# Moving eight of sixteen low-part subtractions from VectorE to GpSimd in a routed expert MLP

## The reference

```python
# block 1: four experts, chosen by token id; Wg = Wu = Wd = ctx_2048 (4 x 512 x 512)
for e in range(E):
    g = jax.nn.silu(jnp.einsum('bsd,fd->bsf', hidden_states, Wg[e]))
    u = jnp.einsum('bsd,fd->bsf', hidden_states, Wu[e])
    y = jnp.einsum('bsf,df->bsd', g * u, Wd[e])
    out = jnp.where((expert_ids == e)[..., None], y, out)
x = x + jnp.tanh(g_xattn[0]) * experts(_layernorm(x), ids, ctx_2048, ctx_2048, ctx_2048)
# block 2: ternary MLP of 1408 hidden channels, scaled per channel
x = x + jnp.tanh(g_ffn[0]) * ffn(_layernorm(x), gate_w, up_w, down_w, gate_s, up_s, down_s)
```

## Time and profile before

| | |
|---|---|
| median of 3 runs | 389.07 us |
| the profiled execution | 389.44 us |
| its span | 387.7 us |
| PE busy | 373.1 us, 96% of the span |
| VectorE busy | 243.5 us, 63% |
| ScalarE busy | 147.1 us, 38% |
| GpSimd busy | 81.8 us, 21% |

### The profile page before, as it was taken

One profiled execution on the slowest core, in us unless ns is written; L12 is line 12 of the kernel. 1 busy time (PEld: TensorE's weight loads), 2 busy tenths in 40 slices (PEclk: granted clock), 3 DMA queues, 4 the chain that ended last, 5 costly groups with the idle time before them and its releaser, 6 DMA issues.

```text
span 387.7 us, 5617 instructions
## 1 busy us (share of the span) xinstructions
PE 373.1 (96%) x1757; PEld 303.1 (78%) x1757; DVE 243.5 (63%) x455; ACT 147.1 (38%) x265; POOL 81.8 (21%) x108
## 2 busy tenths in 40 slices
PE   3999999999999999999999999999999999999992
PEld 2477788888888878888888888888888888888891
DVE  6888856667877678778847255747246757222253
ACT  4355556565545346422332223332222332222220
POOL 7523443434352120010002101002101001200011
PEclk9999999999999999999999999999999999999997
DMA  6775666663221126333201322200232300100011
GB/s 221 258 253 191 248 216 253 210 216 102 89 68 68 56 86 216 97 119 81 83 0 54 135 80 83 71 11 31 88 124 62 101 27 27 81 0 0 0 41 73
DMA packets 21905, 40.91 MB, mean 106 GB/s; under 512 B 2672, under 2 KB 8816, under 8 KB 21888
## 3 DMA queue, kind: packets, MB, share of 16 engines
q1 hardware_dynamic: 17536, 26.50, 21.3%
q0 software_dynamic: 4352, 14.19, 9.8%
HBM read 28.36 MB, written 12.32 MB: 105 GB/s over the span
## 4 chain that ended last, share of the span: by engine, by line
PE 93%; DVE 3%; POOL 1%; issue 1%; ACT 0%; DVEq 0%; POOLq 0%
PE bank L1149 40%; PE bank L1045 26%; PE bank L1156 20%; PE bank L1031 2%; PE bank L1060 2%; PE bank L1073 1%; POOL minus_j L362 1%; PE bank L1021 0%; DVE rows L934 0%; PE bank L1012 0%; DVE tmp L927 0%; DVE xn L927 0%; DVE is_low L647 0%; PE bank L1083 0%; DVE sh L882 0%
## 5 line engine op out<-in xcount | busy, mean ns | idle before, releaser
L1149 PE MATMUL bank<-work,wgu 128*128 (+1 forms) x736 | 167.3, 380 | 0.0
L1149 PEld LDWEIGHTS bank<-work,wgu 128*128 128x128 f32 x736 | 133.9, 188 | 27.1 <-issue 0.5
L1045 PE MATMUL bank<-work,parts 128*128 (+1 forms) x432 | 110.7, 402 | 0.8 <-ACT parts L463 0.2
L1045 PEld LDWEIGHTS bank<-work,parts 128*128 128x128 f32 x432 | 78.5, 188 | 20.0 <-issue 2.9
L1156 PE MATMUL bank<-work,hp 128*128 128x512 f32 x352 | 87.2, 390 | 0.2 <-DVE hp L886 0.2
L1156 PEld LDWEIGHTS bank<-work,hp 128*128 128x128 f32 x352 | 65.7, 188 | 14.4 <-DVE hp L886 0.6
L867 DVE SCALAR_TENSOR_TENSOR sh<-bank,gs,sh 128x512 f32<-128x512 f32 x42 | 31.5, 749 | 55.6 <-PE bank L1149 55.6
L567 ACT ACTIVATE hp<-sh 128x512 fp32r<-128x512 f32 x42 | 26.6, 634 | 78.7 <-DVE sh L867 78.7
L562 ACT ACTIVATE sh<-bank,gs 128x512 f32<-128x512 f32 x42 | 28.9, 689 | 71.6 <-PE bank L1149 68.8
L391 POOL TENSOR_TENSOR rstd<-ve,half 128x1 f32<-128x1 f32 x31 | 18.1, 583 | 124.3 <-DVE ve L708 124.3
L446 POOL DMA_INDIRECT out<-rows,oidx x16 | 16.2, 1011 | 128.0 <-DVE rows L934 105.8
(11 more groups left out here) (132 smaller groups left out, 267.4 us busy)
## 6 DMA issues: line engine op xcount, KB each, us to landing
wraw<-guT SPq DMA_DIRECT2D x8, 704.0 KB
ctx_in<-ctxT SPq DMA_DIRECT2D x4, 1024.0 KB, 6.1
rows<-x_rows SPq DMA_DIRECT2D x8, 512.0 KB, 4.4
turned_rows<-xn SPq DMA_DIRECT2D x12, 256.0 KB, 2.7
rows<-turned_rows SPq DMA_DIRECT2D x12, 256.0 KB, 2.7
checked<-dwT SPq DMA_DIRECT2D x11, 256.0 KB
rows<-dwT SPq DMA_DIRECT2D x11, 256.0 KB, 2.9
rows<-x,gidx POOLq DMA_INDIRECT x19
```

Source lines behind the costliest of these rows:

```text
L1045: mm = pe.matmul(out_ps[:, :], part(s)[:, c * P:(c + 1) * P], ctx_w(e, c, w), start=n == 0, stop=n == last)
L1149: mm = pe.matmul(out_ps[:, tiles.start * P:tiles.stop * P], wgu[:, row + h, w, c * P:(c + 1) * P], moving, start=n == 0, stop=n == last)
```

## The change

Eight of the sixteen low parts are made by GpSimd: (e, c) = (0,3), (1,3), all four of expert 2, and (3,0), (3,1). VectorE keeps (0,0), (0,1), (0,2), (1,0), (1,1), (1,2), (3,2), (3,3). The instruction is the same, a `tensor_tensor` subtraction of 128 x 512. GpSimd's go into its queue after gather 3 (one), after gather 4 (one), after gather 5 and ahead of inverse_std(3) (four), and after store 0 (two). On VectorE, step 1 begins with three subtractions, step 2 has none, and step 3 has two, which moved behind h_lo(2). TensorE and SyncE wait on two semaphores in place of one.

```diff
+ON_POOL = [(0, 3), (1, 3), (2, 0), (2, 1), (2, 2), (2, 3), (3, 0), (3, 1)]
+ON_VECTOR = [(e, c) for e in range(EXPERTS) for c in range(KC) if (e, c) not in ON_POOL]
...
-            sp.wait_ge(S["ctx_lo"], EXPERTS * KC)
+            sp.wait_ge(S["ctx_lo"], len(ON_VECTOR))
+            sp.wait_ge(S["pool_ctx_lo"], len(ON_POOL))
...
+            def ctx_lo(n):
+                e, c = ON_POOL[n]
+                pool.wait_ge(S["ctx_hi"], KC * e + c + 1)
+                pool.tensor_tensor(ctx_w(e, c, 1), ctx_in[:, e, c, :], ctx_w(e, c, 0).bitcast(F32),
+                                   ALU.subtract).then_inc(S["pool_ctx_lo"], 1)
...
             gather(3)
+            ctx_lo(0)
             inverse_std(1)
             gather(4)
+            ctx_lo(1)
             inverse_std(2)
             pool.wait_ge(S["early_row"], 16)
             gather(5)
+            for n in range(2, 6):
+                ctx_lo(n)
             inverse_std(3)
             pool.wait_ge(S["tables_ready"], 2)
             pool.wait_ge(S["rows_ready"], 1)
             store(0)
+            for n in range(6, len(ON_POOL)):
+                ctx_lo(n)
...
             def step_with_ctx(k):
-                ctx_lo(KC * k, KC * (k + 1))
+                if k == 1:
+                    ctx_lo(3, 6)
                 norm(k + 1, ring_slot(k + 1))
                 h_lo(k - 1)
+                if k == 3:
+                    ctx_lo(6, 8)
                 hidden(k)
...
-            ctx_lo(2, KC)
+            ctx_lo(2, 3)
             norm(1, ring_slot(1))
...
-                    if n >= 2 * KC and ctx_ready:
-                        pe.wait_ge(S["ctx_lo"], ctx_ready - KC + c + 1)
+                    if n >= 2 * KC and ctx_of is not None:
+                        pe.wait_ge(*ctx_low_ready(ctx_of, c))
```

More of the change, by code:

```diff
@@ L246, in build @@
             z_done y_done silu_ready h_ready ht_done early_index early_row xn_out xq_in xt_ready hhi_ready hlo_ready u_done rows_ready
-            scaled gates_ready dsb_ready ctx_hi ctx_lo out_stored  held
+            scaled gates_ready dsb_ready ctx_hi ctx_lo pool_ctx_lo out_stored  held
             check_landed sums_done checks_done loose_step loose_ready loose_counted flag_ready
@@ L778, in ctx_lo @@
             def ctx_lo(n_from, n_to):
-                for n in range(n_from, n_to):
-                    e, c = n // KC, n % KC
-                    dve.wait_ge(S["ctx_hi"], n + 1)
+                for e, c in ON_VECTOR[n_from:n_to]:
+                    dve.wait_ge(S["ctx_hi"], KC * e + c + 1)
                     dve.tensor_tensor(ctx_w(e, c, 1), ctx_in[:, e, c, :], ctx_w(e, c, 0).bitcast(F32),
@@ L1032, in turn_x, with ctx_low_ready, expert_product @@
                 mm.then_inc(S["xt_done"], 1)
-            def expert_product(out_ps, part, e, hi_ready, lo_ready, ctx_ready=None):
+            def ctx_low_ready(e, c):
+                made, sem = (ON_POOL, "pool_ctx_lo") if (e, c) in ON_POOL else (ON_VECTOR, "ctx_lo")
+                return S[sem], made.index((e, c)) + 1
+            def expert_product(out_ps, part, e, hi_ready, lo_ready, ctx_of=None):
                 last = len(PASSES) * KC - 1
@@ L1050, in expert, with first_product @@
                 return pe.value_load(tiles[0:1, 0, ds(k, 1)], min_val=0, max_val=EXPERTS - 1)
-            def first_product(k, e=None, ctx_ready=None):
+            def first_product(k, e=None, ctx_of=None):
                 e = expert(k) if e is None else e
                 expert_product(z_ps, tile_x, e, (S["xhi_ready"], k + 1),
-                               (S["xlo_ready"], k + 1), ctx_ready).then_inc(S["z_done"], 1)
+                               (S["xlo_ready"], k + 1), ctx_of).then_inc(S["z_done"], 1)
             def turn_h(k):
@@ L1078, in _ @@
             keep_busy(3)
-            first_product(0, 0, ctx_ready=KC)
+            first_product(0, 0, ctx_of=0)
             pe.wait_ge(S["low_ready"], 3)
@@ L1091, in _, with expert_step @@
             turn_h(0)
-            def expert_step(k, e=None, e_before=None, ctx_ready=None, first=None):
-                first_product(k, e, ctx_ready)
+            def expert_step(k, e=None, e_before=None, ctx_of=None, first=None):
+                first_product(k, e, ctx_of)
                 turn_x(k + 1)
@@ L1106, in _ @@
             for k in range(1, EXPERTS):
-                expert_step(k, *experts_at(k), ctx_ready=KC * (k + 1))
+                expert_step(k, *experts_at(k), ctx_of=k)
             with pe.Fori(EXPERTS, 15) as k:
```

## The result

The changed kernel takes 394.75 us (median of 4 runs, 394.34 to 395.38) against 389.1 us before: ratio 1.0151, 95% interval 1.0136 to 1.0165, so 5.65 us slower. The forecast was 387.3 us.

The account below looks back on a forecast made before the run. TensorE was taken as the bound, with 3.02 us to win in first products 0 to 3. Gains of 0.19 us, then totals of 0.58, 1.28 and 1.78, gave 387.3 us from the median; range 386.6 to 389.2.

Parts of the forecast that it names:

- The price of one subtraction: Time of one 128 x 512 subtraction on GpSimd, estimated from memset and select: 1.3 us, low end 0.88, high end 2.1.
- Step 0: Product 0, with (0,3) on GpSimd and (0,2) waiting for it: last matmul at 19.34 instead of 19.53, gain 0.19 us.
- Step 1: Product 1, with (1,3) on GpSimd: ends at 25.58 us instead of 26.16, total gain 0.58.
- The first rival: GpSimd's (2,0) goes ahead of norm(2), which stands still 1.3 us: total gain only 0.62, 388.45 us; chance 0.32.
- Step 2: Product 2, with no VectorE subtraction ahead of it: its 0.70 us over go, total gain 1.28 us.
- the forecast slack: Margin for norm(3), held behind GpSimd's four until 31.7 us, with turn_x(3) due at 32.1: 0.4 us.
- Step 3: Product 3, with (3,0) and (3,1) on GpSimd: a stall of 0.1 remains of 0.61; gain 0.5 us, total 1.78.
- The carry-over: After the start, TensorE is busy 234.83 of 235.00 us, so the rest takes over any gain or loss one for one.

## Why the prediction was wrong

- **The price of one subtraction** was right: 1.28 us on GpSimd (1.255 to 1.306) for a forecast 1.3, worked out from a memset and a select.
- **Step 0** came near in its total, and partly by luck: product 0 ended at 19.94 instead of 20.03, 0.09 us early for a forecast 0.19. It was shorter than forecast (3.19 us, forecast 3.35), but began 0.26 us later than before (16.75 against 16.49); over the traces of all these kernels its start lies between 16.09 and 17.00, which the sum held fixed. (0,2) did not meet (0,3), which ended at 18.18, ahead of it. In five of the six traces in which product 0 began at 16.09 to 16.16 they met, as forecast: (0,2) took 0.77 us in one and 0.92 or 0.93 in four. (A reading was slightly off: the power instruction of the earlier trace rows ended 0.43 us after the first subtraction, 19.30 against 18.87, and not 0.5. The sum does not use it.)
- **Step 1 is where it failed.** The sum let "the three subtractions of VectorE end at 22.84 + 0.60 + 0.60 + 0.68 = 24.72", so it put the wait of (1,2) at nothing and gave no reason. The first rival had GpSimd ahead of norm(2), for one instruction of 1.3 us. I looked for a meeting only at norm(2): by the sum (1,2) began at 24.04, ahead of the end of gather 5 at 24.2 to 24.39. In fact (1,2) was the victim, took 5.86 us and ended at 29.99: being shown to begin first did not protect it, and the hold lasted for the row of four. Forecast: 0.58 us gained by the end of product 1, or by the rival 0.58 lost. Measured: turn_x(2) 5.18 us late.
- **The clock** was in no term. After the wait of 5.24 us TensorE was granted 0.50; between turn_x(2) and turn_h(1) the delay grows from 5.18 to 6.99 us (36.43 against 29.44), and with the gap filled some 2 us are back.
- **Step 2** was right, in mechanism and size: product 2 lasts 2.75 us in place of 3.48 (a gain of 0.73 for a forecast 0.70), and the delay falls from 6.99 to 6.26. GpSimd had been ready with its four 7 us before that product began, so this trace doesn't test the forecast slack; the kernel that waits for norm(2) does, and there the product takes 2.78.
- **Step 3** had the right mechanism and too large a size: 0.14 us gained in the product (3.25 against 3.39) for a forecast 0.5. (3,3) comes at 45.88, 2.61 us after the product's start, for a computed 2.56; but a matmul that starts after a wait, alone, has 0.49 us in the chain and not 0.23, so that even a stall of 0.11 costs nearly 0.4.
- **The carry-over** was right: 5.92 us of delay at turn_x(4) and 5.79 at the end.

With the two engines kept apart by one wait the forecast sum nearly comes out: 1.6 us by the ratio for 1.78. In the chain 0.45 us are gained at turn_x(2), 1.22 at turn_x(3) and 1.57 at turn_x(4), for a forecast 0.58, 1.28 and 1.78. The sum was nearly right for a kernel in which the two engines don't meet from step 1 on; the meeting was known as a risk and priced with the wrong victim and a quarter of the length.

## What to carry to other kernels

Before work is moved to GpSimd beside VectorE, list every VectorE instruction with two SBUF inputs, and those like norm (one SBUF input, but 0.54 us where a subtraction of the size takes 0.68), that can fall into the time of GpSimd's whole row. Count that time from the indirect DMA ahead of the row to its last instruction, and price the meeting with the rest of the row. Where it can't be excluded, put GpSimd's row behind a semaphore of VectorE's last such instruction: that one wait was worth 7 us here. Waits inside the row are the second choice: with them the kernel was still 1.6 us slower than before by the ratio. A stall on TensorE of a few microseconds has to be priced with the lower clock behind it, here about 2 us for a wait of 5.2.

## What the runs showed of the hardware

- GpSimd's row behind an indirect DMA can stop a VectorE instruction that is shown to begin ahead of it: victims shown to begin 0.38, 0.42 and 0.70 us ahead stood until the row was over, while others shown to begin 0.99 and 1.03 us ahead were not held up. With a semaphore wait between the gather and the row, one that began 0.38 us ahead wasn't either.
- Nine norms that began inside an indirect DMA with no row behind it took 0.54 to 0.58 us.
- VectorE's victim ends 0.56 us behind an unbroken row where it is a two-input subtraction, and 0.28 to 0.31 us behind it where it is a norm.
- GpSimd's memsets of 128 x 512 (four in 1.94 us) stop a norm and not a two-input subtraction; VectorE instructions with one SBUF and one PSUM input ran in their usual time beside GpSimd's subtractions (0.68 us for the changed (1,2), 0.69 and 0.68 for hidden(2) and x_lo(3) of the changed kernel beside the row at 39.20 to 41.74 us).
